# First scan of a state-space layer: the B term formed on TensorE, and steps cut by channel block instead of by half sequence

## The reference

```
proj = x @ W_in + b_in;  x_ssm, x_gate = split(proj)
x_conv = silu(causal_depthwise_conv(x_ssm))
Bm, Cm = split(x_conv @ W_bc + b_bc)            # 16 states each
dt = softplus(x_conv @ W_dt + b_dt);  A = -exp(A_log)
def step(h, (xt, dtt, Bt, Ct)):                 # over 1024 tokens
    dA = exp(dtt[:, :, None] * A)
    h  = h * dA + (dtt * xt)[:, :, None] * Bt[:, None, :]
    y  = einsum('bdn,bn->bd', h, Ct) + xt * D
out = (y * silu(x_gate)) @ W_out + b_out;  layernorm(out + x)
```

## Time and profile before

| | |
|---|---|
| median of 3 runs | 3328.77 us (3325.11 to 3330.94) |
| profiled execution | 3329.13 us; its span, first to last instruction, 3327.4 us |
| busy in the span | PE 83%, DVE 73%, ACT 40%, POOL 19% |
| mean granted clock of PE | 0.906 of full (2.4 GHz) |
| first scan, scan 0 to the gate's second half | 96.70 to 258.43 us |

### The profile page before, as it was taken

One profiled execution on the slowest core, in us unless ns is written; L12 is line 12 of the kernel. 1 busy time (PEld: TensorE's weight loads), 2 busy tenths in 40 slices (PEclk: granted clock), 3 DMA queues, 4 the chain that ended last, 5 costly groups with the idle time before them and its releaser, 6 DMA issues.

```text
span 3327.4 us, 36552 instructions
## 1 busy us (share of the span) xinstructions
PE 2758.6 (83%) x12264; PEld 1576.6 (47%) x12264; DVE 2433.5 (73%) x4936; ACT 1339.7 (40%) x2455; POOL 622.2 (19%) x426
## 2 busy tenths in 40 slices
PE   4226888997889997889998888992369999999998
PEld 2003764444665344665345764441135656566564
DVE  6996687997687997678998586006877676776766
ACT  2323326773425773424773325553640131411313
POOL 2444000332100333100233000001000040310404
PEclk9557899998989998989998989996669999999999
DMA  5001000001000001000001000006020000000000
GB/s 159 0 0 45 1 1 7 23 20 53 1 1 5 22 20 57 1 1 1 23 23 46 10 0 7 23 20 127 0 34 1 1 14 1 1 14 1 14 1 13
DMA packets 57635, 65.93 MB, mean 20 GB/s; under 512 B 27757, under 2 KB 46690, under 8 KB 56802
## 3 DMA queue, kind: packets, MB, share of 16 engines
q1 hardware_dynamic: 57441, 63.51, 7.1%
HBM read 45.22 MB, written 9.88 MB: 17 GB/s over the span
## 4 chain that ended last, share of the span: by engine, by line
PE 59%; DVE 25%; issue 5%; ACT 4%; POOL 2%; DMA 1%; SPq 0%; DVEq 0%; ACTq 0%; POOLq 0%
PE psum L1712 14%; PE psum L383 8%; DVE arena L543 6%; PE psum L938 4%; PE psum L1772 3%; PE psum L790 3%; PE psum L1052 3%; DVE arena L538 3%; PE psum L956 3%; PE psum L770 2%; PE psum L373 2%; PE psum L374 2%; PE psum L269 2%; PE psum L781 2%; PE psum L1071 1%
## 5 line engine op out<-in xcount | busy, mean ns | idle before, releaser
L1712 PE MATMUL psum<-weights,arena 128*128 128x384 f16 x3072 | 534.9, 329 | 5.1 <-DVE arena L2068 4.0
L383 PE MATMUL psum<-arena,weights 128*128 128x512 f32 (+1 forms) x1024 | 522.6, 593 | 5.0 <-ACT arena L457 5.0
L2071 DVE SCALAR_TENSOR_TENSOR arena<-psum,arena 128x384 f32<-128x384 f32 x480 | 295.7, 616 | 193.7 <-PE psum L1712 182.6
L457 ACT ACTIVATE arena<-psum,minus_scale 128x512 f32<-128x512 f32 x512 | 350.7, 686 | 215.1 <-PE psum L383 213.3
L1712 PEld LDWEIGHTS psum<-weights,arena 128*128 128x128 f16 x3072 | 304.2, 99 | 194.3 <-issue 8.8
L598 POOL TENSOR_TENSOR arena<-arena 128x1024 f32<-128x1024 f32 x128 | 274.0, 2141 | 598.6 <-DVE arena L543 598.0
L543 DVE TENSOR_TENSOR_SCAN arena<-weights,arena 128x1026 f32<-128x1026 f32 x128 | 293.9, 2296 | 18.4 <-ACT weights L450 3.8
L246 POOL TENSOR_SCALAR shifted<-mean_var 128x4 f32<-128x4 f32 x40 | 9.8, 245 | 1287.1 <-DVE mean_var L223 1287.1
L1947 POOL TENSOR_TENSOR arena<-arena 128x512 f32<-128x512 f32 x112 | 147.6, 1321 | 509.8 <-ACT arena L1886 499.2
L383 PEld LDWEIGHTS psum<-arena,weights 128*128 128x128 f32 (+1 forms) x1024 | 166.1, 163 | 98.7 <-ACT arena L457 12.1
L450 ACT ACTIVATE weights<-arena,weights 128x512 f32<-128x512 f32 x256 | 169.1, 712 | 102.8 <-DVE arena L543 102.8
(11 more groups left out here) (324 smaller groups left out, 4867.0 us busy)
## 6 DMA issues: line engine op xcount, KB each, us to landing
arena<-arena SPq DMA_DIRECT2D x64, 128.0 KB, 2.3
arena<-head_inv SPq DMA_DIRECT2D x32, 256.0 KB, 3.4
weights<-in_qkv SPq DMA_DIRECT2D x2, 3072.0 KB, 17.1
weights<-gate_upT_kept SPq DMA_DIRECT2D x4, 1408.0 KB, 6.4
x_all<-in_x SPq DMA_DIRECT2D x4, 1024.0 KB, 11.9
weights<-in_cWkv SPq DMA_DIRECT2D x4, 1024.0 KB, 11.3
out<-x_all SPq DMA_DIRECT2D x4, 1024.0 KB, 4.4
weights<-downT_kept SPq DMA_DIRECT2D x4, 640.0 KB, 7.0
```

Source lines behind the costliest of these rows:

```text
L383: pe.matmul(psum[0:rows, 3 + turn % 2, :], value_and_ones(kt, hd), expd[:, i % 2, :], start=kt == 0, stop=kt == NT - 1).then_inc(pv2_done, 1)
L457: a.activation(expd[:, i % 2, :], psum[:, i % 3, :], ACT.Exp, bias=minus_scale[:, :], scale=SCALE / QK ** 2).then_inc(exp_done, 1)
L1712: last = pe.matmul(psum[:, n % PROJ_BANKS, 0:W3], zT_parts[:, of_z, c, k * P:(k + 1) * P], w_parts[:, c, e, of_w, :], start=c == 0 and j == 0,
L2071: step_ = v.scalar_tensor_tensor(qkv[:, k, :], src, router_w[:, k, e:e + 1], qkv[:, k, :], ALU.mult, ALU.add)
```

## The change

For the first scan alone, four new functions take the place of the `loop_...` functions. A step is now one state s and one channel block m (j = 2s + m) over all 1024 tokens.

- The B term u * B is formed by PE: u is transposed once, so that tokens lie on the partitions (`uT`, 2 x 8 tiles of 128 x 128), and B too (`bT`). For each state ACT makes eight diagonal matrices diag(B[s, tokens]) of 128 x 128 (`diagonals`, a ring of two states), and PE multiplies each tile of uT by its diagonal matrix (`input_row`): eight f32 products of 128 x 128 fill a row of 1024 in two PSUM banks. Rows take turns in banks 0, 1 and 2, 3.
- The spread C of a state is one row of 1024 in two banks (`c_row`), used by both of its steps.
- The scan reads dA from SBUF and its input from PSUM. There is no end state to hand on.
- POOL's add waits for the C product alone. Both halves of the gate are at the end.

```diff
+        r = Region(arena, after_parts)
+        h_row = r.take(RING, T)
+        uT, bT = r.take(DC, NT, P), r.take(NT, 2 * N_STATE)
+        diag = Region(arena, scan_end).take(2, NT, P)
+        dA_row = Region(weights, slot_end - RING * 2 * (HALF + 1)).take(RING, T)
...
-                own(v.tensor_scalar(bc[:, j * HALF:(j + 1) * HALF], psum[0:96, j, :], b_bc, None, ALU.add))
+                step = v.tensor_scalar(bc[:, j * HALF:(j + 1) * HALF], psum[0:96, j, :], b_bc, None, ALU.add)
+                if alone:
+                    own.bring(step, bc_kept, j + 1)
+                else:
+                    own(step)
...
+        def row_at(j, first):
+            return psum[:, first + 2 * (j % 2):first + 2 * (j % 2) + 2, :].rearrange("p b x -> p (b x)")
+
+        def first_scan_pe(pe):
+
+            def turn_u(m):
+                pe.wait_ge(u_ready, m + 1)
+                for k in range(NT):
+                    last = pe.transpose(psum[:, 4 + 2 * m + k // 4, (k % 4) * P:(k % 4 + 1) * P],
+                                        u[:, m, k * P:(k + 1) * P], ident[:, :])
+                    if k % 4 == 3:
+                        last.then_inc(uT_psum, 1)
+
+            def input_row(j):
+                s, m = j // DC, j % DC
+                pe.wait_ge(diag_made, NT * (s + 1))
+                if s == 0:
+                    pe.wait_ge((uT_kept_0, uT_kept_1)[m], 2)
+                if j >= 2:
+                    pe.wait_ge(scan_done, j - 1)
+                for k in range(NT):
+                    last = pe.matmul(psum[:, 2 * (j % 2) + k // 4, (k % 4) * P:(k % 4 + 1) * P], uT[:, m, k, :],
+                                     diag[:, s % 2, k, :], start=True, stop=True)
+                last.then_inc(ub_psum, 1)
+
+            def c_row(s):
+                if s >= 2:
+                    pe.wait_ge(p_done, 2 * (s - 1))
+                else:
+                    pe.wait_ge((uT_kept_0, uT_kept_1)[s], 2)
+                for half in range(2):
+                    last = pe.matmul(psum[:, 4 + 2 * (s % 2) + half, :], select[0:96, N_STATE + s, :],
+                                     split[0:96, half * HALF:(half + 1) * HALF], start=True, stop=True)
+                last.then_inc(c_psum, 1)
+
+            pe.wait_ge(bc_kept, 2)
+            for k in range(NT):
+                last = pe.transpose(psum[:, 2, 2 * N_STATE * k:2 * N_STATE * (k + 1)],
+                                    bc[0:2 * N_STATE, k * P:(k + 1) * P], ident[0:2 * N_STATE, 0:2 * N_STATE])
+            last.then_inc(bT_psum, 1)
+            turn_u(0)
+            turn_u(1)
+            pe.wait_ge(bT_kept, 1)
+            for s in range(N_STATE):
+                input_row(2 * s)
+                c_row(s)
+                input_row(2 * s + 1)
+
+        def first_scan_act(a):
+
+            def diagonals(s):
+                if s >= 2:
+                    a.wait_ge(ub_psum, 2 * (s - 1))
+                for k in range(NT):
+                    a.activation(diag[:, s % 2, k, :], ident[:, :], ACT.Copy,
+                                 scale=bT[:, k, s:s + 1]).then_inc(diag_made, 1)
+
+            def decay_row(j):
+                s, m = j // DC, j % DC
+                if s == 0:
+                    a.wait_ge(dt_ready, m + 1)
+                if j >= RING:
+                    a.wait_ge(scan_done, j - RING + 1)
+                a.activation(dA_row[:, j % RING, :], dt[:, m, :], ACT.Exp,
+                             scale=a_neg[:, m, s:s + 1]).then_inc(da_ready, 1)
...
+            diagonals(0)
+            decay_row(0)
+            for g in range(2):
+                a.wait_ge(uT_psum, 3 + g)
+                a.activation(uT[:, 1, 4 * g:4 * g + 4, :].rearrange("p k x -> p (k x)"), psum[:, 6 + g, :],
+                             ACT.Copy).then_inc(uT_kept_1, 1)
+            decay_row(1)
+            for s in range(1, N_STATE):
+                diagonals(s)
+                decay_row(2 * s)
+                decay_row(2 * s + 1)
+
+        def first_scan_dve(v, own):
+            for g in range(2):
+                v.wait_ge(uT_psum, g + 1)
+                v.tensor_copy(uT[:, 0, 4 * g:4 * g + 4, :].rearrange("p k x -> p (k x)"),
+                              psum[:, 4 + g, :]).then_inc(uT_kept_0, 1)
+            for j in range(STEPS):
+                row = h_row[:, j % RING, :]
+                if j >= RING:
+                    v.wait_ge(y_added, j - RING + 1)
+                v.wait_ge(da_ready, j + 1)
+                v.wait_ge(ub_psum, j + 1)
+                v.tensor_tensor_scan(row, dA_row[:, j % RING, :], row_at(j, 0), 0.0, ALU.mult,
+                                     ALU.add).then_inc(scan_done, 1)
+                v.wait_ge(scan_done, j + 1)
+                v.wait_ge(c_psum, j // DC + 1)
+                v.tensor_tensor(row, row, row_at(j // DC, 4), ALU.mult).then_inc(p_done, 1)
+            v.wait_ge(y_added, STEPS)
+            for half in range(2):
+                gate_half(v, own, half)
+
+        def first_scan_pool(g):
+            g.wait_ge(y_begun, DC)
+            for j in range(STEPS):
+                g.wait_ge(p_done, j + 1)
+                if j >= DC:
+                    g.wait_ge(y_added, j - 1)
+                g.tensor_tensor(y[:, j % DC, :], y[:, j % DC, :], h_row[:, j % RING, :], ALU.add).then_inc(y_added, 1)
+            g.wait_ge(y_added, STEPS)
...
-            loop_pe(pe, False, True)
+            first_scan_pe(pe)
...
-            a.wait_ge(u_ready, DC)
-            loop_act(a, False, True)
+            first_scan_act(a)
...
-            loop_pool(g, False, True)
+            first_scan_pool(g)
...
-            front(0)
-            loop_dve(v, own, False, True)
+            front(0, alone=True)
+            first_scan_dve(v, own)
```

More of the change, by code:

```diff
@@ L207, in program @@
         Norm = namedtuple("Norm", "stat mean_var rstd shifted stats_ready shifted_ready rstd_ready")
+        bc_kept, bT_psum, bT_kept, uT_psum, uT_kept_0, uT_kept_1, diag_made, ub_psum = (
+            cx_psum, cx_squared, cx_summed, cx_root, cx_scaled, cx_high, cx_split, cx_turned)
         by_stage = Norm(stat, mean_var, rstd, shifted, stats_ready, shifted_ready, rstd_ready)
@@ L485, in loop_act, with front_dve @@
                 head_keep(a, 2 * CH - 1)
-        def front_dve(v, own, between=None):
+        def front_dve(v, own, between=None, alone=False):
             for m in range(DC):
@@ new lines, in first_scan_act @@
+        def first_scan_act(a):
[13 more added lines that the diff above has]
+                             scale=a_neg[:, m, s:s + 1]).then_inc(da_ready, 1)
+            a.wait_ge(bT_psum, 1)
+            a.activation(bT[:, :, :].rearrange("p k s -> p (k s)"), psum[:, 2, 0:2 * N_STATE * NT],
+                         ACT.Copy).then_inc(bT_kept, 1)
+            a.wait_ge(bT_kept, 1)
+            diagonals(0)
[9 more added lines that the diff above has]
+                decay_row(2 * s + 1)
@@ L2574, in _, with front @@
             v.wait_ge(inputs_in, 16 * B)
-            def front(b, between=None):
+            def front(b, between=None, alone=False):
                 own(v.memset(xs[:, :, 0:D_CONV - 1], 0.0))
                 norm_x(v, own, b, 0, 0, own_stats=True, to=of_scan)
-                front_dve(v, own, between)
+                front_dve(v, own, between, alone)
             def batch(b, scan):
```

## The result

The changed kernel takes 3287.98 us (median of 4 runs, 3286.06 to 3288.64) against 3328.01 us for the kernel before (4 runs beside them, 3325.11 to 3330.94). The ratio is 0.9879 with an interval of 0.9867 to 0.9891: faster by 1.2%, 40.0 us. The forecast was 3284.8 us, its range 3279 to 3300. The profiled execution of the changed kernel took 3286.06 us (span 3284.3), 43.1 less than that of before.

A forecast was written before the change was run, and what follows sets the result against it. VectorE was taken to bound the first scan. Scan 0 at 99.5, 31 steps of 3.47 us and the end put L660 at 215.25 instead of 259.57: 3329.1 - 44.3 = 3284.8 us, range 3279 to 3300.

The forecast's parts named there:

- The step: In the first scan's loop VectorE does only scan and C product: 2.33 + 1.14 = 3.47 us, bounds 3.44 and 3.68.
- The PSUM operand: The scan reading its B term from PSUM was counted as costing nothing; the skill's figures gave 65 ns per scan.
- third rival: The scan runs slower with PSUM as source: at the bound 1.21 us per step, 38.7 us lost, 3323.5 us; chance 0.04.
- PE beside VectorE: PE's rows of B terms, 1.8 to 2.0 us at full clock, 3.5 to 3.7 at half, were taken as hidden.
- first rival: PE becomes the scan's bound, its clock staying at half or falling back: step 3.9 us, 3298.6 us; chance 0.10.
- fourth rival: PE's weight load and product don't overlap for the B rows: step 7.8 us at half clock, kernel 3423 us; chance 0.02.
- The add beside the scan: POOL's add, now let go by the C product, runs beside the next scan and was counted as costing it nothing.
- second rival: Scan and POOL's add shut each other out: 2.0 us per step, 64 us, 3348.8 us; chance 0.06.
- Start and end: First scan at 99.5 us, 2.8 later than before; L660 4.6 us after the last C product instead of 4.5.
- The bounds given: For the first scan's start: 96.9 us at full clock, 100.5 at half clock with a second wait of a microsecond.
- The sum: Start, steps and end put L660 at 215.25 instead of 259.57, 44.3 us less, so 3284.8 us for the kernel.
- behind L660 stands the same work in the same order, so it goes straight to the end: After the scan and gate, the 44.3 us gained up to L660 were to shorten the whole kernel by as much.

The follow-up runs named there:

- shape alone: Changed kernel with the B product back on VectorE, u not turned, no diagonals, POOL's add waiting for the next scan: 3322.43 us, ratio to before 0.9989.
- rows formed twice: Changed kernel with PE forming every row of B terms two times over into the same place: 3297.80 us, ratio to before 0.9913.
- add held back: Changed kernel with POOL's add waiting until the next scan is over, as before the change: 3287.14 us, ratio to before 0.9886.
- products on POOL: Changed kernel with 7 of the 32 C products moved from VectorE to POOL, ACT copying their spread C to SBUF: 3276.71 us, ratio to before 0.9844.
- changed, again: The changed kernel, unaltered, measured once more on another chip: 3287.25 us, ratio to before 0.9874.
- two ends: Changed kernel with PE forming row 0 before turning u's second half, ACT copying both halves from PSUM, VectorE adding the last product: 3283.79 us, ratio 0.9866.
- both together: Changed kernel with the edits of two ends and of products on POOL combined: 3278.67 us, ratio to before 0.9852.
- shape alone, add let go: The shape alone kernel without POOL's wait for the next scan, so its add meets a scan with both operands in SBUF: 3355.96 us, ratio 1.0095.

## Why the prediction was right

**The step.** Predicted 3.47 us, measured (206.94 - 99.91) / 31 = 3.453: over 31 steps 0.6 us less. The two durations it was put together from, 2.33 from scan to product and 1.14 from a product to an instruction that doesn't wait for it, came out as 2.31 and 1.14.

**The PSUM operand.** Taken as free from the products; the scan takes 2.28 us with it and 2.29 without (the shape alone). The 65 ns per scan estimated from the Trainium skill (VectorE: DVE Perf Modes, "The TRN2 errata") don't show in this trace, and the third rival falls.

**PE beside VectorE.** A row was put at 1.8 to 2.0 us at full clock and 3.5 to 3.7 at half; it took 1.95 to 2.02 and 3.62. The clock rose as argued from the stretches elsewhere, in work without a pause, and stayed up. The first rival would have cost 0.43 us per step; rows formed twice brought PE to its bound and cost 0.34, so PE's work does come onto the path once it is longer than a step. That rows at half clock (3.62 us) would have done the same is an inference: a scan with PE held at half clock was not tried. The fourth rival falls with the spacing of 0.112 to 0.126 us per instruction.

**The add beside the scan.** Counted at nothing, rightly, and for the reason given, the one operand in SBUF: the scan stays at 2.28 us with the add begun before it. With both operands in SBUF the same meeting cost 1.05 us per scan and turned a gain of 5 us into a loss of 28. The second rival's price, a whole add of 2.0 us per scan, was not what such a meeting costs: 1.05 us came, since the add had run 1.15 us when the scan was issued. A detail was off as well: the add was said to be let go just when the scan starts, and it is issued 0.17 us behind.

**Start and end.** The first scan was forecast 5.58 us behind the end of u (93.92 to 99.5). It came 5.55 behind it: u ended at 94.36 in this execution, 0.44 later than in that of before, and the scan started at 99.91. That the start fits to 0.03 us is partly luck. It rests on a first row wholly at half clock, and where in this row the clock rises differs between executions: with the add held back, the same code up to there, the row took 2.44 us and the first scan came 4.37 us behind u; with the products on POOL 2.50 and 4.43. The bounds given, 96.9 to 100.5, hold all of these. From the last scan to the norm 8.15 us were reckoned and 8.26 measured.

**The sum.** Up to the norm the terms err by +0.44, -0.03, -0.6 and +0.1 us: 215.20 against 215.25. What fell short is the step "behind L660 stands the same work in the same order, so it goes straight to the end". The order is the same, but the stages behind don't take the same time in each execution. Below, each kernel's profiled execution against that of before, at the norm's first instruction (259.57 before) and at the end (3329.13 before):

| kernel | norm starts | earlier by | time | shorter by |
|---|---|---|---|---|
| changed | 215.20 | 44.4 | 3286.06 | 43.1 |
| changed, again | 215.06 | 44.5 | 3289.05 | 40.1 |
| add held back | 214.83 | 44.7 | 3283.37 | 45.8 |
| two ends | 212.29 | 47.3 | 3283.83 | 45.3 |
| products on POOL | 205.49 | 54.1 | 3269.90 | 59.2 |
| both together | 204.44 | 55.1 | 3277.10 | 52.0 |
| rows formed twice | 227.05 | 32.5 | 3304.04 | 25.1 |
| shape alone | 254.02 | 5.6 | 3320.87 | 8.3 |
| shape alone, add let go | 285.47 | -25.9 | 3355.10 | -26.0 |

Between the norm and the end, from -7.4 to +5.1 us come and go, and the first two lines, which are one kernel, differ by 3 us there. One place where these two part is the attention of the second batch. The rows give PE's products there and the reciprocal of VectorE that waits for them, in the first execution of the changed kernel and then in the other, and under each pair the stretch around it with the granted clock (the last number but two).

```profile
1328.98 4.37 PE L914 MATMUL psum<-arena 77*128 77x68 f32 x32 [0.68 <-ACT arena L977]
...
1333.39 0.26 DVE L1017 RECIPROCAL arena<-psum 128x16 f32<-128x16 f32 x1 [2.86 <-PE psum L914]
```

```profile
1328.00:1336.00 8.00, 7.32 (x41) 6.20 (x40) 3.18 (x4) 2.16 (x3) 0.00 (x0) 0.75 0.00 0
```

```profile
1330.53 5.70 PE L914 MATMUL psum<-arena 77*128 77x68 f32 x31 [0.68 <-ACT arena L977]
...
1336.47 0.26 DVE L1017 RECIPROCAL arena<-psum 128x16 f32<-128x16 f32 x1 [5.18 <-PE psum L914]
```

```profile
1331.00:1339.00 8.00, 8.00 (x36) 7.21 (x36) 0.97 (x3) 1.23 (x1) 0.00 (x0) 0.57 0.00 0
```

The same products take 4.37 us in one and 5.70 in the other, and 3.1 us lie between the reciprocals, where 0.1 us lay between the norms. The products are 1.3 of these 3.1, and the distance isn't steady: the same instructions of VectorE stand 0.1 us apart up to 1267 us of the first execution, 1.7 at 1279 (granted clock from 1272 to 1280 us 0.88 and 0.67), under 0.1 at 1318, 1.5 at 1345, and 3.2 to 3.3 from 1356 to past 2000. So at these places the stages behind give and take some microseconds by the spells in which PE's clock is at its lower level, in one and the same kernel. For the other lines of the table this was not followed. Whether an earlier start of these stages also shifts the spells by rule, and so holds part of the 4.4 us between 44.4 and 40.0, stays open.

## What to carry to other kernels

When one engine is full, add up what stands on it from start to start, with the gap that a waiting and an unwaiting successor leave (1.35 and 1.14 us in this case): the step was forecast to 0.02 us before it existed. Where work goes to another engine, ask where its result lands: an operand in PSUM made the scan deaf to POOL's adds, where two in SBUF cost 1.05 us per step. Of the gain in an early stage count on what is left at its end, and give the later stages their scatter in the range.

## What the runs showed of the hardware

- A scan with both operands in SBUF that is issued while POOL's add runs all but stands until the add is over (3.34 us instead of 2.29); the add keeps its 2.35. With one operand in PSUM the scan takes 2.28 beside the same add. Beside POOL's product with a column, a scan with both operands in SBUF took 2.55.
- Two scans that don't wait for one another start 2.20 us apart and take 4.46 us together, one alone 2.28.
- POOL's add of 128x1024 f32 takes 2.33 to 2.38 us in every kernel with the new tiles, beside scans or beside products. Over the old ones most took 2.00, but every third took 2.36, always that of the same one of the ring's three buffers, with the same shape and the same kind of work beside it. So it goes with the buffer, and the two pieces of 512 alone don't decide it. What about the buffer's place does it is open.
- The chain of work that ended last can name the wrong releaser where two engines were freed by one event. In the changed kernel it reads:

```profile
102.23 1.16 ACT weights L684
103.39 2.27 DVE arena L714
```

The decay on ACT at 102.23 was let go by the end of scan 0, so it is step 3's (a ring of three), and the scan at 103.39 (103.37 on VectorE's own list) is step 1's. The scan follows the C product, 1.14 us behind its start; the decay ended within 0.02 us of that.
